# Attention block on one Trainium2 core: the first unit's start in another order, padded key rows

## The reference, cut to what matters

```python
def xattn(q, k, v, mask, W_Q, W_K, W_V, W_T):          # q = layernorm(x), k = v = ctx
    Q, K, V = split_heads(q @ W_Q), split_heads(k @ W_K), split_heads(v @ W_V)
    score = jnp.einsum('bhqd,bhkd->bhqk', Q, K) / math.sqrt(8)
    score = jnp.where(mask == 0, -1e9, score)
    out = jnp.einsum('bhqk,bhkd->bhqd', jax.nn.softmax(score, axis=-1), V)
    return merge_heads(out) @ W_T
x = x + jnp.tanh(g_xattn[0]) * xattn(layernorm(x), ctx, ctx, mask, ...)
x = x + jnp.tanh(g_ffn[0]) * ffn(layernorm(x), w1, w2, router_w)    # top-2 of 8 experts
```

## Time and profile before

| | us |
|---|---|
| Median of 3 runs | 435.59 |
| Lowest, highest | 435.38, 442.27 |
| The profiled execution | 435.39 |
| Its span in the trace | 433.7 |
| TensorE busy in it | 409.1 |
| First score starts at | 44.58 |

### The profile page before, as it was taken

How to read it: one execution, slowest core, us unless ns; L and a number is a source line. 1 busy time by engine, 2 the same in 40 slices (tenths; PEclk the granted TensorE clock), 3 DMA queues, 4 the chain that set the end, 5 groups by cost and what they waited for, 6 DMA issues and landing times.

```text
span 433.7 us, 10135 instructions
## 1 busy us (share of the span) xinstructions
PE 409.1 (94%) x3747; PEld 237.3 (55%) x3747; DVE 321.7 (74%) x693; ACT 273.5 (63%) x575; POOL 120.3 (28%) x266
## 2 busy tenths in 40 slices
PE   7988899999999999999999999999997898999995
PEld 3435355545554555455555555555543576777884
DVE  3990878677677899888889988888995572443785
ACT  3403656677676777777776777777774467666333
POOL 4716753436333015000001510000133000000275
PEclk9998999999999999999999999999998899999999
DMA  8768845449566732405142240504223343646122
GB/s 291 168 148 148 195 146 122 169 87 329 151 180 232 196 69 56 93 10 102 31 84 61 66 86 16 101 17 97 49 54 116 111 127 93 186 126 184 30 56 63
DMA packets 31806, 50.37 MB, mean 116 GB/s; under 512 B 3612, under 2 KB 20188, under 8 KB 31756
## 3 DMA queue, kind: packets, MB, share of 16 engines
q1 hardware_dynamic: 29684, 47.53, 42.7%
q0 software_dynamic: 768, 1.57, 1.1%
q10 hardware_dynamic: 1304, 0.59, 0.5%
HBM read 36.00 MB, written 13.44 MB: 114 GB/s over the span
## 4 chain that ended last, share of the span: by engine, by line
PE 75%; DVE 11%; DMA 5%; issue 2%; ACT 2%; POOL 2%; SPq 2%; DVEq 0%; POOLq 0%
PE banks L1491 21%; PE banks L1466 20%; PE banks L1448 16%; PE banks L1538 4%; DVE chunk_max L1065 4%; PE banks L1560 3%; DVE chunk_max L1047 3%; DMA queries<-neg_rows 3%; PE banks L1340 2%; PE banks L1548 2%; PE banks L1568 1%; PE banks L1334 1%; DMA probs<-x 1%; ACT probs L910 1%; DVE late L1249 1%
## 5 line engine op out<-in xcount | busy, mean ns | idle before, releaser
L1065 DVE TENSOR_REDUCE chunk_max<-banks 128x1 f32<-128x512 f32 (+1 forms) x390 | 239.2, 665 | 64.8 <-PE banks L1448 63.7
L910 ACT ACTIVATE probs<-banks 128x512 f32<-128x512 f32 x384 | 210.1, 601 | 77.2 <-PE banks L1466 76.6
L1466 PE MATMUL banks<-queries,keys 75*128 75x256 bf16 (+1 forms) x832 | 158.7, 275 | 2.4 <-DMA queries<-neg_rows 1.7
L1448 PE MATMUL banks<-keys,queries 72*128 72x512 bf16 x480 | 145.3, 335 | 1.3 <-DVE chunk_max L1065 1.0
L1466 PEld LDWEIGHTS banks<-queries,keys 75*128 75x128 bf16 (+1 forms) x832 | 72.5, 100 | 74.2 <-issue 15.1
L1491 PE MATMUL banks<-probs,value_t 128*9 128x256 f32 x1536 | 98.4, 382 | 0.0
L1491 PEld LDWEIGHTS banks<-probs,value_t 128*9 128x9 f32 x1536 | 34.8, 90 | 45.3 <-ACT probs L910 12.1
L1448 PEld LDWEIGHTS banks<-keys,queries 72*128 72x128 bf16 x480 | 42.3, 97 | 14.0 <-DVE chunk_max L1065 4.2
L651 POOL COPY value_t<-values 128x384 f32<-128x384 f32 x16 | 8.0, 503 | 116.1 <-PE banks L1491 112.9
L1249 DVE SCALAR_TENSOR_TENSOR late<-late,banks 128x256 f32<-128x256 f32 x35 | 14.6, 417 | 19.2 <-ACT late L934 18.5
L712 POOL TENSOR_SCALAR neg_max<-row_max 128x8 f32<-128x8 f32 x16 | 3.8, 240 | 80.5 <-DVE row_max L1042 80.2
(11 more groups left out here) (178 smaller groups left out, 349.4 us busy)
## 6 DMA issues: line engine op xcount, KB each, us to landing
keys<-k_parts SPq DMA_DIRECT2D x48, 300.2 KB
keys<-w SPq DMA_DIRECT2D x19, 384.0 KB, 3.3
slot_x<-ctx_in SPq DMA_DIRECT2D x5, 704.0 KB, 4.3
ctx_in<-ctxT SPq DMA_DIRECT2D x3, 800.5 KB, 10.0
k_parts<-split SPq DMA_DIRECT2D x6, 400.2 KB, 8.8
k_parts<-late SPq DMA_DIRECT2D x6, 400.2 KB, 6.7
queries<-q_parts SPq DMA_DIRECT2D x16, 144.0 KB
w<-w SPq DMA_DIRECT2D x1, 2048.0 KB, 12.4
```

Of the source, the lines that this page charges most:

```text
L910: nc.scalar.activation(probs[:, s % (HELD * QH), :], ring[ring_bank["scores", n]][:, :], ACT.Exp, scale=SCALE).then_inc(probs_ready, 1)
L1065: nc.vector.reduce_max(dst, src, axis=AX.X).then_inc(chunk_used, 1)
L1448: last = nc.tensor.matmul(dst[:, i * CW[c]:(i + 1) * CW[c]], queries[q][0:ROWS, j, t * P:(t + 1) * P], keys[q][0:ROWS, j, c * BANK:c * BAN ...
L1466: last = nc.tensor.matmul(dst, keys[q][0:KR, j, t * P:t * P + w], queries[q][0:KR, j, :], start=True, stop=not with_mask)
```

## The change

- x is loaded in two pieces. Only the two tiles of batch 0 are normed and transposed at the start. The other six (`FIRST_TILES` onward) are normed on VectorE in slots 0, 1, 2, 4 and 5 of unit 0 (`normalise_rest`), with GpSimd's roots in slot 3, and are transposed as two new pieces of kind X.
- The mask is compared in three parts (`MASK_CUTS`): the first 512 columns of tile 0, the rest of tile 0, and tile 1 after the first quad's reduction.
- The count of masked entries moves from TensorE to ScalarE: two copies of 1601 columns with an accumulated sum, stored to DRAM and loaded back as one row, which VectorE reduces before the last quad's reduction.
- The order at the start: keys chunk 0, both query projections, keys chunk 1, quad 0, keys chunks 2 and 3, then the other quads in a new order with the short ones in the middle. Six warm-up matmuls instead of ten.
- A key row has 1632 columns instead of 1601 in DRAM and SBUF (3264 bytes for 3202); the scores still use 1601.
- Nine stores of unit 0's query parts move from ScalarE's queue to SyncE's, between the three key stores; the load of batch 1's ctx moves behind the loads of units 0 and 1.
- The first six chunks of unit 1 run before the first score, three of them before `neg_transpose`; the four value projections of batch 0 stand between the others. In the slots of unit 0 the lead grows by six instead of twelve.
- No pieces run ahead any more: 28 pieces (two of them X) stand in the slots, seven a unit.
- The stores of the other queries and of batch 1 to 3's key parts, batch 3's ctx, the zero fills and the load of x for the tail get fixed places (`stage`, `ZERO_AT`, `S_X_B`).

```diff
-SK = 1601
+SK, SKP = 1601, 1632
-QUADS = [(t, c) for t in range(QT) for c in range(CH - 1)] + [(t, CH - 1) for t in range(QT)]
+QUADS = [(0, c) for c in range(CH)] + [(1, CH - 1)] + [(1, c) for c in range(CH - 1)]
-LEAD = 12
+MASK_CUTS = [(0, 0, BANK), (0, BANK, SK), (1, 0, SK)]
+FIRST_TILES = QT
+LEAD, CHUNKS_FIRST = 12, 6
-RAMP = 10
+RAMP = 6
-PIECE_SLOTS = (4, 7, 12, 14, 21)
-PIECES = ([("Q", 0, 0), ("V", 1, 0), ("V", 1, 1), ("Q", 0, 1), ("V", 1, 2), ("V", 1, 3)] + [("K", 1, i) for i in range(CH)]
-          + [(kind, b, i) for b, kinds in ((2, "VK"), (3, "KV")) for i in range(CH) for kind in kinds])
-AHEAD, AHEAD_COMMON = 7, 2
+PIECE_SLOTS = (1, 4, 7, 12, 14, 20, 22)
+PIECES = [("V", 1, 0), ("K", 1, 0), ("X", 0, 0), ("K", 1, 1), ("X", 0, 1), ("K", 1, 2), ("V", 1, 1),
...
+S_REST, S_RSTD_REST = {0: ("stats", 0), 1: ("stats", 1), 2: ("means", 0), 4: ("norm", 0), 5: ("norm", 1)}, 3
+KEYS_1_AT, CTX_3_AT, Q_REST_AT, KEYS_2_AT, KEYS_3_AT = (1, 8), (1, 16), (1, 23), (3, 1), (4, 3)
+def chunks_ahead(n):
+    return n + min(LEAD, CHUNKS_FIRST + (n + 1) // 2)
...
@@ SyncE
-            sp.dma_start(ctx_in[:, 1, :], ctxT[1]).then_inc(ld_ctx[1], 16)
+            sp.wait_ge(pads_ready, 1)
             for p, made in enumerate((k_hi, k_mid, k_lo)):
                 sp.wait_ge(made, CH)
                 sp.dma_start(k_parts_dram[0, :, p], split0[:, p, :]).then_inc(k_stored[0], 16)
+                if p < 2:
+                    sp.wait_ge(q_cut, 4)
+                    for part, copy in [(part, copy) for part in range(PARTS) for copy in range(PARTS)][5 * p:5 * p + 5]:
+                        sp.dma_start(q_parts_dram[:, part, copy, :, 0:S], q_split[:, part, 0:S]).then_inc(q_stored, 16)
             sp.wait_ge(k_stored[0], 16 * PARTS)
             load_keys(0, 0)
             sp.wait_ge(q_stored, 16 * PARTS * PARTS)
             load_queries(0, 0)
             load_unit(0, 1)
+            sp.dma_start(ctx_in[:, 1, :], ctxT[1]).then_inc(ld_ctx[1], 16)
             sp.wait_ge(neg_rows_ready, 1)
...
@@ ScalarE
+            def count_masked(t):
+                act.wait_ge(mask_used, 2 + t)
+                hold(act, sums_step, t)
+                nc.scalar.activation(mask_copy, masked_q[:, t, :], ACT.Copy, accum_out=mask_sum[:, t:t + 1]).then_inc(sums_step, 1)
+            first_part(0)
+            act.wait_ge(q_proj, 1)
+            nc.scalar.copy(q_rows, q_rows_bank[:, 0:S]).then_inc(q_rows_ready, 1)
+            for c in range(1, CH):
+                first_part(c)
+            for c in range(2):
+                middle_part(c)
+            for t in range(QT):
+                count_masked(t)
+            for c in range(2, CH):
+                middle_part(c)
...
-            act.wait_ge(q_cut, 4)
-            for c in range(PARTS):
-                for p in range(PARTS):
-                    act.dma_start(q_parts_dram[:, c, p, :, 0:S], q_split[:, c, 0:S]).then_inc(q_stored, 16)
...
@@ TensorE
-            pe.wait_ge(quad_used, len(QUADS) - 1)
-            pe.wait_ge(const_ready, 2)
-            for t in range(QT):
-                for c in range(CH):
-                    count = nc.tensor.matmul(count_bank[0:1, 0:CW[c]], ones_col[:, :],
...
-            neg_transpose(0, 0)
-            project_values(0, 2, value_banks[2]).then_inc(v_ready, 1)
-            project_values(0, 3, value_banks[3]).then_inc(v_ready, 1)
...
-                for n in range(AHEAD_COMMON, AHEAD):
-                    hold(pe, piece_out, n + 1 - len(ahead_banks))
-                    project(n, ahead_banks[n % len(ahead_banks)]).then_inc(piece_ready, 1)
-                pe.wait_ge(piece_out, AHEAD)
+                for g in range(3):
+                    chunk(g)
+                pe.wait_ge(quad_used, len(QUADS))
+                neg_transpose(0, 0)
+                pe.wait_ge(ld_wv, 16)
+                for g in range(CH):
+                    first_values(g)
+                    if 3 + g < CHUNKS_FIRST:
+                        chunk(3 + g)
                 pe.wait_ge(v_copied, CH)
```

309 lines of the change are left out of this document (178 added, 131 removed), and 3 rows, old and new, of the table PIECES.

## The result

| | before | after |
|---|---|---|
| Median (runs) | 438.51 (4) | 461.42 (4) |
| Lowest, highest | 435.38, 442.27 | 460.39, 462.55 |
| The profiled execution, its span | 435.39, 433.7 | 460.39, 458.7 |

A forecast was written before the change was run, and what follows sets the result against it. Bounds: key store, loads and 2 KB of maxima up to the first score, then TensorE. First score 4.2, units 1 to 3 5.0 and unit 0 1.5 make 10.7 us on 435.4: 446.1, range 437 to 452.

The forecast's parts named there:

- Start of the loads: Before the first score: third key store issued at 22.5 us for 23.73, so unit loads start 1.2 us earlier.
- Key rows, no gain by padding: Key loads of units 0 and 1: padding rows to 3264 bytes leaves their rate as it is, no gain.
- rival 1: Key loads: padding doubles their rate, keys land 6.0 to 6.5 us earlier, total 439.8 us; chance 0.15.
- sign of 250 to 270 ns a row: Key loads in the changed profile: queue 1 alone with keys again takes 250 to 270 ns a row.
- From the loads to the first score: Chunks, transposition and value projections follow the loads' end at 42.9; first score at 48.8, 4.2 us later than before.
- the term for the clock: Before the first score: TensorE at half speed over 3 us of work after its pause adds 1.5 us.
- Pieces in units 1 to 3: Projection pieces moved into the slots of units 1 to 3 lengthen them by 0.8, 1.5 and 2.7, 5.0 us.
- Unit 0, 1.5 between -1 and +4: Unit 0 grows 1.5 us as the layer norm's rest joins VectorE's slots; -1 only lead's relief, +4 norm wholly in the way.
- Stores and the rest: Zero fills and the moved load of x counted as 0, since SyncE is free there; removed count matmuls also 0.
- Query stores at the end of unit 1: Nine stores ahead of batch 1's first load, needed in unit 2, just fit: counted 0, other end 3 us.
- Rival 2: Units 0 to 3: moved pieces find idle TensorE time, total 440.6 us; chance 0.16.
- rival 3: Kernel start: TensorE keeps half speed until the first quads, third key store at 25, total 450.6 us; chance 0.15.

The follow-up runs named there:

- before_pad: The kernel before with only the key rows padded to 1632 columns, pads set to zero; ratio 1.0003 to before.
- mended: The kernel after with the six tiles' norm and maxima transposition ahead of the first chunks, and key pieces, their store, zero fills and x load re-placed; ratio 1.017 to before.
- keys3: The kernel after with the late key pieces of batches 2 and 3 dealt anew and batch 3's key store moved into unit 3; ratio 1.031 to before.
- before_no_ahead: The kernel before with no pieces ahead of the first score, its 26 pieces in seven slots a unit; ratio 1.007 to before.
- ln_early: The kernel after with the other six tiles' layer norm on VectorE all ahead of the first chunk's reduction; ratio 1.022 to before.
- mended_warm: The run mended plus 44 matmuls on a constant, into banks nobody reads, in TensorE's waits before the first score; ratio 1.016 to before.
- after_again: The kernel after, unchanged, run again on another chip; ratio 1.053 to before.

## Why the prediction was wrong, step by step

Forecast 446.1 (437 to 452), measured 461.4; the direction was right, the range too low by 9 us. On the span: 10.7 forecast, 25.0 measured. The order of the work before the first score and the key rows were foreseen; three terms of the sum were not the size that they were given.

- **Start of the loads, -1.2.** Third store at 22.85 for 22.5: held. But its issue took 1.70 us and its landing 4.60, so the loads came 0.3 earlier.
- **Key rows, no gain by padding.** Held, shown by before_pad; rival 1 fell with it. The sign of 250 to 270 ns a row was a little high: 252 on average before, 238 after.
- **Loads landed at 42.9.** 42.39: held.
- **From the loads to the first score, 5.9 us (48.8).** 8.7 (51.12). The order of the work was right; the term for the clock was mis-sized. Named as 1.5 us, it entered the sum with 0.6, by the middle of 48.8. Without it the text had 48.2 less 42.9, 5.3, which leaves 3.4 for the half clock: it held for the whole stretch, not for "3 us of work". The price of the order is about 5 us (5.1 in mended, with the loads at the same time).
- **Pieces in units 1 to 3, 5.0.** 5.4 measured. But 1.8 of these are the cut of a key piece ahead of `negate`, which the sum didn't have: in keys3 units 1 to 3 are 3.6 us longer than before. before_no_ahead gives 3.5 for the same move, and 2.5 more in unit 0. The size was right partly by luck.
- **Unit 0, 1.5 between -1 and +4.** 7.9. This is the step that failed most. The upper end counted VectorE's busy time ("the layer norm wholly in the way"). That was the wrong account in three ways: the norm itself took twice its time beside GpSimd's cuts; everything queued behind it came late, with TensorE at a full ring; and TensorE, kept waiting, lost its clock. ln_early shows the 7.9. What the clock alone can cost a unit is 3.3 us (mended against mended_warm); in after's unit 0 its share is not set apart, and after_again speaks for a small one. The same norm at the same early place left unit 0 at 31.0 in mended, so the cure depends on the clock too.
- **Stores and the rest, 0, "since SyncE is free there".** 4.8 in unit 4 (mended takes back 4.1 of it by the store, the fills and the load of x). The forecast asked whether SyncE had time, not what memory the load of x goes into nor what wait stands ahead of it, and the third key batch's last piece in slot 22 of unit 3 was never followed to its landing.
- **Query stores at the end of unit 1, 0 to 3.** 0: in keys3 TensorE waits 0.3 us in all for queries from unit 2 to 4.
- **Rival 2** (pieces find idle time) fell with before_no_ahead; **rival 3** (a cold start) didn't happen in after, and did in mended_warm, 3.7 us.

The terms were added up as if independent. They aren't: several of TensorE's waits, not all, put a part of the following work at 1.2 GHz, and most of those waits are what the change made.
The Trainium skill ("TensorE: Matmul & The Clock Gate", Part 1) has the throttled clock as the default state, which activity releases. The forecast drew on it for rival 3 and for the clock before the first score. In the second the trace agrees (13 us without work, then 0.50 for the work behind it), while behind short waits the traces show both levels.
